# New lists of pieces for the Mamba units of a fused Mamba and mixture-of-experts kernel

## What is computed

```python
def mamba2(u, l):                      # l: layer
    z, xBC, dt = split(u @ in_w[l].T)  # 512, 512 + 64 + 64, 8
    dt  = softplus(dt + dt_bias[l])
    xBC = silu(causal_conv4(xBC) + conv_b[l])
    x, B, C = split(xBC)               # x: 8 heads of 64, B, C: 64
    dA = exp(dt * -exp(A_log[l]))
    state = dA * state + (dt * x) B^T  # over the 512 tokens, per head
    y = state C + D[l] * x
    y = y * silu(z)
    return rmsnorm(y) * rms_w[l] @ out_w[l].T
h = x
for l in range(2):
    h = mamba2(layernorm(h) * ln_w[l] + ln_b[l], l) + h
x = layernorm(x + h)
logits = x @ gate_w + gate_b           # 8 experts, top 2, softmax of the two
x = layernorm(x + sum of w_k * expert_k(x))  # (silu(x Wg) * (x Wv)) @ W2
```

## Time and profile before

| | |
|---|---|
| timed runs | 1418.2, 1421.18, 1423.03 us |
| profiled execution, first to last instruction | 1418.7 us |
| TensorE, VectorE, ScalarE, GpSimd busy | 1272.5, 1090.1, 804.2, 791.7 us |
| plain units | 40.3 and 41.1 us by turns |
| routed units | 44.9 us, one of them 49.8 |
| table loads on ScalarE, lines L1221 and L1210 | 16 and 16 |

### The profile page before, as it was taken

One profiled execution on the slowest core, in us unless ns is written; L12 is line 12 of the kernel. 1 busy time (PEld: TensorE's weight loads), 2 busy tenths in 40 slices (PEclk: granted clock), 3 DMA queues, 4 the chain that ended last, 5 costly groups with the idle time before them and its releaser, 6 DMA issues.

```text
span 1418.7 us, 40444 instructions
## 1 busy us (share of the span) xinstructions
PE 1272.5 (90%) x13336; PEld 1050.7 (74%) x13337; DVE 1090.1 (77%) x2560; ACT 804.2 (57%) x1861; POOL 791.7 (56%) x751
## 2 busy tenths in 40 slices
PE   4889999999999999999888799999999999999970
PEld 2456666666667666666678799999999999999960
DVE  4889999999999999899967877565566656565536
ACT  4667666666666776667545344444454544444436
POOL 3467666767675877788774615234072406152772
PEclk9899999999999999999968999999999999999996
DMA  6213432333443233322235231303012312202594
GB/s 211 81 31 120 135 109 93 96 119 119 135 135 120 84 113 117 123 88 81 87 146 189 72 121 34 121 27 122 30 54 94 105 51 76 72 30 63 134 210 162
DMA packets 90547, 145.73 MB, mean 103 GB/s; under 512 B 9376, under 2 KB 73376, under 8 KB 90336
## 3 DMA queue, kind: packets, MB, share of 16 engines
q1 hardware_dynamic: 75104, 97.03, 21.4%
q0 software_dynamic: 15072, 46.51, 11.2%
q10 hardware_dynamic: 288, 1.19, 0.2%
HBM read 103.03 MB, written 41.67 MB: 102 GB/s over the span
## 4 chain that ended last, share of the span: by engine, by line
PE 48%; DVE 25%; issue 12%; POOL 6%; ACT 5%; DMA 1%; DVEq 1%; SPq 0%; ACTq 0%; POOLq 0%
PE pe L1101 12%; PE pa L1101 12%; PE py L1126 11%; DVE arena L1691 5%; DVE arena L1730 4%; POOL arena L2631 3%; PE pa L676 2%; DVE arena L1738 2%; PE pm L853 2%; PE py L815 2%; DVE arena L1757 2%; DVE arena L1744 1%; PE pt L835 1%; DVE arena L1664 1%; DVE arena L1645 1%
## 5 line engine op out<-in xcount | busy, mean ns | idle before, releaser
L1101 PE MATMUL pe<-arena 128*128 128x128 f16 x3408 | 219.4, 220 | 26.0 <-issue 26.0
L1101 PEld LDWEIGHTS pe<-arena 128*128 128x128 f16 x3408 | 203.4, 98 | 31.3 <-issue 30.6
L1101 PE MATMUL pa<-arena 128*128 128x128 f16 x3408 | 218.8, 220 | 0.0
L1553 ACT ACTIVATE arena<-pe,arena 128x128 f32<-128x128 f32 x568 | 162.0, 371 | 79.8 <-PE pe L1101 78.9
L1101 PEld LDWEIGHTS pa<-arena 128*128 128x128 f16 x3408 | 201.5, 98 | 0.0
L1126 PE MATMUL py<-arena 128*128 (+1 forms) x1704 | 197.7, 273 | 1.3 <-DVE arena L2337 0.9
L1691 DVE SCALAR_TENSOR_TENSOR arena<-pa,arena 128x511 f32<-128x511 f32 (+2 forms) x240 | 178.9, 746 | 11.6 <-ACT arena L1199 5.5
L1126 PEld LDWEIGHTS py<-arena 128*128 128x128 f16 x1704 | 163.4, 98 | 19.6 <-issue 1.8
L2300 DVE SCALAR_TENSOR_TENSOR pm<-pa,arena 128x128 f32<-128x128 f32 x284 | 80.5, 352 | 98.7 <-ACT arena L1553 88.0
L1730 DVE TENSOR_TENSOR_SCAN arena<-arena,pe 128x512 f32<-128x512 f32 x128 | 148.8, 1204 | 3.2 <-issue 1.8
L2531 POOL TENSOR_SCALAR arena<-arena 128x1536 f16<-128x1536 f32 (+2 forms) x35 | 42.6, 1218 | 189.3 <-DVE arena L2337 184.1
(11 more groups left out here) (309 smaller groups left out, 2539.5 us busy)
## 6 DMA issues: line engine op xcount, KB each, us to landing
arena<-step_rows SPq DMA_DIRECT2D x64, 512.0 KB, 6.3
arena<-in_w_exp POOLq DMA_DIRECT2D x32, 768.0 KB, 4.8
arena<-queue SPq DMA_DIRECT2D x74, 129.5 KB, 2.1
answer<-arena SPq DMA_DIRECT2D x71, 128.0 KB, 1.7
arena<-in_x SPq DMA_DIRECT2D x16, 512.0 KB, 6.2
answer<-zeros SPq DMA_DIRECT2D x10, 512.0 KB, 4.8
arena<-h SPq DMA_DIRECT2D x9, 512.0 KB, 5.5
h<-arena SPq DMA_DIRECT2D x8, 512.0 KB, 3.0
```

The lines of the kernel that those rows point to most:

```text
L1101: ins = pe.matmul(bank[:, f * P:(f + 1) * P], w_split[:, p, hl, d * 2 * FF + col:d * 2 * FF + col + P], x[:, r, d, :], start=(n == 0), sto ...
L1553: ins = e.activation(sg[:, half, f, :], GATE[half][:, f * P:(f + 1) * P], ACT.Silu, bias=b1a[:, bass.ds(ex_, 1), ff], scale=1.0 / S1)
```

## The change

Only the order of the calls changes in the functions `plain`, `routed` and `final` on four engines. No piece is added or taken away, and no piece's own code changes. `prologue`, `first`, `epilogue`, SyncE's queue and the expert part stay. Below are the list of `plain` and the parts of `routed` and `final` that matter here, cut from the diff; the printed functions above hold the old lists whole. In `routed`, ScalarE's `x1_apply` now stands behind `conv_silu` of c3 and `z_silu` 0.

On TensorE:

```diff
 def plain(st):
     c = [Chunk(st, k) for k in range(NK + 1)]
-    chunk_a(c[1])
     do_fills(st, ["dt"])
     chunk_cb(c[1])
+    chunk_a(c[1])
     do_fills(st, ["c4"])
     do_fills(st, ["c0"])
     chunk_s(c[0])
...
     steps(st.u + 1, 1 - st.q)
     do_fills(st, ["c1"])
     chunk_c(c[0])
+    chunk_y(c[1])
     chunk_s(c[1])
-    chunk_y(c[1])
+    chunk_a(c[2])
     do_fills(st, ["c2"])
-    chunk_a(c[2])
     chunk_z(c[2])
     chunk_d(c[0])
     chunk_cb(c[2])
     do_fills(st, ["c3"])
+    chunk_c(c[1])
     chunk_s(c[2])
     turn_b(st.u + 1, 1 - st.q, c[0].n + 1)
-    chunk_c(c[1])
     do_fills(st, ["z0"])
+    chunk_a(c[3])
     chunk_y(c[2])
+    chunk_cb(c[3])
+    do_fills(st, ["z2"])
     chunk_d(c[1])
-    chunk_a(c[3])
-    chunk_cb(c[3])
     do_fills(st, ["z1"])
-    do_fills(st, ["z2"])
+    chunk_z(c[3])
     do_fills(st, ["ln0"])
     chunk_c(c[2])
-    chunk_z(c[3])
     chunk_y(c[3])
+    chunk_cb(c[4])
+    do_fills(st, ["ln1"])
     chunk_a(c[4])
-    do_fills(st, ["ln1"])
     chunk_d(c[2])
     chunk_c(c[3])
-    chunk_cb(c[4])
     do_fills(st, ["z3"])
     chunk_d(c[3])
...
 def final(st):
     c = [Chunk(st, k) for k in range(NK)]
     chunk_y(c[0])
+    chunk_s(c[0])
+    chunk_cb(c[1])
     chunk_a(c[1])
-    chunk_cb(c[1])
-    chunk_s(c[0])
+    chunk_z(c[1])
     chunk_c(c[0])
-    chunk_z(c[1])
+    chunk_d(c[0])
     chunk_cb(c[2])
     do_fills(st, ["t0"])
-    do_fills(st, ["t1"])
-    chunk_y(c[1])
-    chunk_d(c[0])
     chunk_a(c[2])
     chunk_s(c[1])
```

On ScalarE:

```diff
 def plain(st):
...
     softplus(st)
     chunk_a(c[1])
     conv_first(st, "c4")
+    first_state(c[0])
     conv_first(st, "c0")
-    first_state(c[0])
+    conv_silu(st, "c4")
+    steps(st)
+    conv_first(st, "c1")
+    squares(c[0])
     chunk_c(c[0])
-    steps(st)
-    conv_silu(st, "c4")
-    conv_first(st, "c1")
+    chunk_a(c[2])
     conv_silu(st, "c0")
-    chunk_a(c[2])
     conv_first(st, "c2")
+    squares(c[1])
     conv_silu(st, "c1")
-    squares(c[0])
     chunk_d(c[0])
     conv_silu(st, "c2")
+    chunk_c(c[1])
     conv_first(st, "c3")
+    z_silu(st, 0)
+    b_rows(st)
+    chunk_a(c[3])
+    ln_apply(st.u + 2, st.q)
+    squares(c[2])
+    z_silu(st, 1)
+    z_silu(st, 2)
+    chunk_c(c[2])
+    ln_out(st, "ln0")
+    conv_silu(st, "c3")
+    chunk_d(c[1])
+    ln_out(st, "ln1")
+    chunk_a(c[4])
+    squares(c[3])
+    chunk_c(c[3])
+    chunk_d(c[2])
+    z_silu(st, 3)
+    chunk_d(c[3])
+
+def routed(st):
+    c = [Chunk(st, k) for k in range(NK + 1)]
+    chunk_a(c[1])
+    softplus(st)
+    conv_first(st, "c4")
+    end_scale(st)
+    first_state(c[0])
+    conv_first(st, "c0")
+    chunk_c(c[0])
+    squares(c[0])
+    conv_silu(st, "c4")
+    chunk_a(c[2])
+    steps(st)
+    conv_first(st, "c1")
+    chunk_d(c[0])
+    conv_silu(st, "c0")
+    chunk_c(c[1])
+    conv_first(st, "c2")
+    b_rows(st)
+    conv_silu(st, "c1")
+    conv_first(st, "c3")
+    chunk_d(c[1])
...
-def routed(st):
-    c = [Chunk(st, k) for k in range(NK + 1)]
-    softplus(st)
-    chunk_a(c[1])
-    conv_first(st, "c4")
-    first_state(c[0])
-    end_scale(st)
-    conv_first(st, "c0")
-    squares(c[0])
-    chunk_c(c[0])
-    steps(st)
-    conv_silu(st, "c4")
-    chunk_d(c[0])
-    chunk_a(c[2])
-    conv_silu(st, "c0")
-    conv_first(st, "c1")
-    conv_first(st, "c2")
-    b_rows(st)
-    chunk_c(c[1])
-    conv_silu(st, "c1")
-    conv_first(st, "c3")
-    x1_apply(st)
-    h_out(st, 0)
```

On VectorE:

```diff
 def plain(st):
     c = [Chunk(st, k) for k in range(NK + 1)]
     scan(c[1])
+    ch1 = Chain(dve, c_dve2, S1_LINKS, st.u + 1)
     dt_first(st)
     chunk_mix(c[1])
-    ch1 = Chain(dve, c_dve2, S1_LINKS, st.u + 1)
     dt_last(st, ch1)
     scan(c[2])
     taps(st, "c4", ch1)
     chunk_b2(c[0])
     chunk_b1(c[1])
+    end_b(st)
     taps(st, "c0", ch1)
-    weigh(st)
-    end_b(st)
     g_low(c[0])
     chunk_b2(c[1])
     next_state(c[1])
...
     chunk_b1(c[2])
     taps(st, "c2", ch1)
     chunk_mix(c[2])
+    next_state(c[2])
+    g_low(c[1])
     ln_stats(st.u + 2, st.h + 1, st.q)
-    g_low(c[1])
     taps(st, "c3", ch1)
     ch1.close()
     chunk_b2(c[2])
-    next_state(c[2])
     scan(c[3])
+    weigh(st)
     chunk_mix(c[3])
     chunk_b1(c[3])
     g_low(c[2])
     chunk_b2(c[3])
     scan(c[4])
+    chunk_mix(c[4])
     g_low(c[3])
-    chunk_mix(c[4])
...
...
     c = [Chunk(st, k) for k in range(NK)]
     scan(c[1])
     chunk_b2(c[0])
+    choose_lead()
     chunk_mix(c[1])
-    choose_lead()
+    g_low(c[0])
+    chunk_b1(c[1])
     end_add(st)
-    chunk_b1(c[1])
-    g_low(c[0])
```

On GpSimd:

```diff
 def plain(st):
+    end(st)
     c = [Chunk(st, k) for k in range(NK + 1)]
+    x_dt(c[1])
+    x_w(c[1])
+    scatter_before(st, 0, 1)
+    gated(c[0])
+    scatter_before(st, 3, 4)
+    old_state(c[1])
+    scatter_before(st, 1, 2)
+    x_d(c[1])
+    scatter_before(st, 5, 6)
+    add_xd(c[1])
+    scatter_before(st, 2, 3)
+    x_dt(c[2])
+    old_state(c[2])
+    gated(c[1])
+    x_w(c[2])
+    x_d(c[2])
+    add_x(st)
+    add_xd(c[2])
+    rsqrt_ln(st.u + 2)
+    x_dt(c[3])
+    scatter_before(st, 6, 7)
+    gated(c[2])
+    x_d(c[3])
+    add_xd(c[3])
+    u_low(st.u + 2, st.q, st, "ln0")
+    scatter_before(st, 4, 5)
+    scatter_before(st, 7, 8)
+    gated(c[3])
+    x_dt(c[4])
+    x_w(c[4])
+    u_low(st.u + 2, st.q, st, "ln1")
+    x_d(c[4])
+
+def routed(st):
+    c = [Chunk(st, k) for k in range(NK + 1)]
+    end(st)
+    x_dt(c[1])
     scatter_before(st, 0, 1)
     x_w(c[1])
     scatter_before(st, 1, 2)
-    scatter_before(st, 2, 3)
+    gated(c[0])
+    scatter_before(st, 5, 6)
     old_state(c[1])
-    end(st)
...
-    c = [Chunk(st, k) for k in range(NK + 1)]
-    end(st)
-    scatter_before(st, 0, 1)
-    scatter_before(st, 1, 2)
-    scatter_before(st, 2, 3)
-    x_w(c[1])
-    x_dt(c[1])
-    gated(c[0])
-    scatter_before(st, 3, 4)
...
 def final(st):
     c = [Chunk(st, k) for k in range(NK)]
...
     gated(c[0])
     x_w(c[1])
     x_dt(c[1])
+    old_state(c[1])
     x_d(c[1])
+    first_weights()
     add_xd(c[1])
-    old_state(c[1])
-    first_weights()
+    old_state(c[2])
+    x_w(c[2])
+    gated(c[1])
     x_dt(c[2])
-    gated(c[1])
-    x_w(c[2])
     x_d(c[2])
-    old_state(c[2])
     rsqrt_x1(st)
     add_xd(c[2])
+    x_dt(c[3])
+    gated(c[2])
+    x_d(c[3])
     scatter_before(st, 0, 2)
-    gated(c[2])
-    x_dt(c[3])
-    x_d(c[3])
     scatter_before(st, 2, 3)
     add_xd(c[3])
     scatter_before(st, 3, 6)
+    scatter_before(st, 6, 8)
     gated(c[3])
-    scatter_before(st, 6, 8)
 def epilogue(st):
```

More of the change, by code:

```diff
@@ new lines, in routed @@
+            def routed(st):
[9 more added lines that the diff above has]
+                conv_silu(st, "c4")
+                chunk_a(c[2])
+                steps(st)
[7 more added lines that the diff above has]
+                conv_first(st, "c3")
+                chunk_d(c[1])
+                squares(c[1])
+                h_out(st, 0)
+                conv_silu(st, "c2")
@@ L1413, in plain @@
                 chunk_a(c[3])
-                z_silu(st, 1)
+                h_out(st, 1)
                 squares(c[2])
                 conv_silu(st, "c3")
+                z_silu(st, 0)
+                x1_apply(st)
+                z_silu(st, 1)
+                ln_apply(st.u + 2, st.q)
                 chunk_c(c[2])
                 z_silu(st, 2)
+                gap_tanh(st)
+                chunk_a(c[4])
                 ln_out(st, "ln0")
-                chunk_a(c[4])
-                ln_out(st, "ln1")
@@ L1466, in routed @@
                 chunk_c(c[3])
                 ln_out(st, "ln1")
-                chunk_d(c[2])
-                squares(c[3])
                 z_silu(st, 3)
@@ L1479, in final @@
                 h_out(st, 0)
+                chunk_a(c[2])
+                squares(c[0])
+                chunk_c(c[1])
+                chunk_d(c[0])
                 h_out(st, 1)
-                squares(c[0])
-                chunk_d(c[0])
-                chunk_a(c[2])
-                chunk_c(c[1])
+                chunk_a(c[3])
                 x1_apply(st)
+                gap_tanh(st)
+                high_parts(0)
+                high_parts(1)
                 squares(c[1])
-                chunk_a(c[3])
-                high_parts(0)
+                chunk_d(c[1])
+                squares(c[2])
                 chunk_c(c[2])
-                squares(c[2])
-                high_parts(1)
-                gap_tanh(st)
-                chunk_d(c[1])
                 e.preload_act_table_set("sqrt_and_others")
+                high_parts(2)
+                squares(c[3])
                 root_out(c[2].q, 0, 3)
                 chunk_c(c[3])
-                squares(c[3])
+                chunk_d(c[2])
                 root_out(c[3].q, 3, NK)
-                chunk_d(c[2])
-                high_parts(2)
             def epilogue(st):
@@ L2022, in routed @@
                 g_low(c[0])
+                ch3 = s3_stats(st)
                 chunk_b1(c[1])
```

(20 more changed lines are left out.)

139 lines of the change are left out of this document (41 added, 98 removed).

## The result

| | before | after |
|---|---|---|
| median of the timed runs | 1419.76 us (1418.2 to 1423.03, 4 runs) | 1473.78 us (1470.98 to 1476.06, 4 runs) |
| ratio to before | | 1.0369, 95% interval 1.0346 to 1.0393 |
| span of the profiled execution | 1418.7 | 1474.4 |
| mean granted clock of TensorE | 0.965 | 0.933 |
| table loads on ScalarE in the Mamba units | 32 | 60 |

What follows compares the result with a forecast made beforehand. A TensorE-VectorE loop, both nearly full, bounds the Mamba units. Plain +6.2, clock +9.6, routed +3.6, final -3 make +16.4; with 1418.7 and 2.5, about 1437 us; range 1413 to 1455.

Steps and rivals of the forecast that it cites:

- So g_low0 waits 1.0: Plain units: VectorE's g_low of chunk 0 waits 1.0 us for ScalarE, held up by a new table load.
- from the end of VectorE's taps c4: Plain units: counted from there, ScalarE needs 6.9 us until g_low of chunk 0 can start, VectorE 5.9.
- rival 3: ScalarE, conv_silu c4 to steps: no load or covered, g_low0's copy within 5.9 us of taps c4; 1412 to 1415, chance 0.17.
- 2.6 was forecast: Plain units: TensorE waits 2.6 us before a2 (transposes of chunk 2), against 0.72 before the change.
- 40.7 + 0.8: Plain unit: +1.1 TensorE, -1.3 VectorE, +1.0 table load make +0.8 us each, +6.2 over eight.
- I take half of the eight: TensorE's clock falls after the wait in half of the eight plain units, 2.4 us each: +9.6.
- rival 2: TensorE's clock falls in every plain unit: 1447 us, up to 1458 where it stays low longer; chance 0.12.
- dense work on both sides of the wait: Plain units: dense work around TensorE's wait spoke against the one row where a similar wait lowered the clock.
- +3.6 was forecast: Six routed units: -0.35 for a wait gone, +0.9 for loads and gated, about +0.6 each; bounds -2 and +8.
- -3 was forecast: Final unit: the last gated on GpSimd comes 2 to 4 us earlier, so -3; bounds -5 and +2.
- choose_lead goes ahead of mix1: Final unit: with this, first_weights is issued some 4 us sooner, but GpSimd's last gated sets the end.
- no scan waits for a step row: Routed units: step rows go out some 8 us later, yet land 5 us before the next unit's scan1.

Runs made afterwards that it cites:

- e4: The changed kernel with ScalarE's steps ahead of conv_silu c4 in the plain and routed lists, so the 28 extra table loads go: 1473.35 us, ratio 1.0354.
- e5: The changed kernel with TensorE computing s1 (chunk_s of chunk 1) six times instead of once in each plain unit: 1450.79 us, ratio 1.0187.
- e8: The changed kernel with GpSimd's plain wait for end_b (1443.39 us), plus TensorE's steps and cb of chunk 2 back ahead of z1 in routed: 1433.9 us.
- e9: The changed kernel with GpSimd's plain wait for end_b, plus TensorE's s1 ahead of fills c1 and c2 in routed: 1444.29 us, ratio 1.0176.

## Why the prediction was wrong, point by point

- **The direction, slower, was right; its main reason was wrong.** "So g_low0 waits 1.0" for ScalarE's table load. The 28 loads came as forecast, but g_low waits nothing, and without them the time is the same (e4). The step that failed is the count "from the end of VectorE's taps c4" with conv_silu c4 at 3.24, load included: ScalarE had nothing left to do at 237.34, so the load ahead of Silu ran beside the taps, which ended at 238.59. Only the load before the Exp counts, and the 6.9 us were 5.6 (to 244.15), less than VectorE's 5.9. That was rival 3's condition, and it held.
- **A term was missing: the price of a moved piece beside its new neighbour.** VectorE's end_b was entered at its old 2.60, while its place and that of three GpSimd products were both moved. It took 4.53. The trace before could have warned: the 2.68 of the earlier trace rows already stood beside an add, which took 1.50 where 1.27 is usual. The +1.0 put down to the loads and the +1.93 of the contention (4.53 for 2.60) act at the same place, so the timetable came out near by luck: a wait of 3.2 at a2, where 2.6 was forecast, and 41.6 for a unit at full clock (e5), where 40.7 + 0.8 was.
- **The clock: mechanism right, size too small.** "I take half of the eight", 2.4 us each, +9.6. It fell in all eight, rival 2, and cost 2.7 in each of the six middle ones, 21.1 in all by e5's profile; e5 gave back 23. The argument that dense work on both sides of the wait would hold the clock had no row behind it. Rival 2's 1447 with the two misses below, 15 and 10, is 1472; but that sum hides that rival 2, too, had a load in g_low's way and no collision.
- **Routed units: +3.6 was forecast, +18.6 measured.** The step counted ScalarE's loads and a delay of 0.1 to 0.2 by GpSimd's gated. It never asked what TensorE had done in gated's time, though the prediction's own show the one long wait of this kind, 2.61 at c(0) before 569.22. The list took steps and cb2 out of that place, and in two units dt_last now stands 1.67 us longer beside x_w, which no term held either; so the one long wait became three. e8 puts steps and cb2 back and gains 9.5, half of the 18.6. The collision's share is read from the trace (a wait of 2.78 with it, 1.03 without) and was not tested by a run.
- **Final unit: -3 was forecast, +7.3 measured.** "choose_lead goes ahead of mix1" was named and given no price. It is 5.15 us of VectorE in front of g_low of chunk 0, and TensorE's d0 waits 3.60 for that. The estimate also had no term for the clock, and the 7.3 are that term: behind this wait TensorE ran 30.7 us at half clock. In e9, where it did not, the same list took 52.9, 3.1 less than the 56.0 of before. That does not confirm the -3, for e9's final unit had 20.9 us at half clock and that of before 34.1.
- **Right:** no scan waits for a step row. They leave SyncE by 585.9 and take 6.5 to land, 4 us before the next unit's scan at 596.42; 5 were forecast. The waits before weigh (265.23) and before g_low of chunk 3 (273.51) are gone.
- **The range** ended at 1455 because rival 2's 1458 was its only bad case. It kept routed and final at their forecast values; their own upper bounds, +8 and +2, were not added to it, and both were too low.

What stays open: what a routed list without dt_last's collision would take, and what decides whether a wait is followed by half clock, above all in the final unit.

## What to carry to other kernels

When a list is reordered, enter each piece at the price that it has beside its new neighbours, not at its old one: a VectorE instruction on two SBUF operands and a GpSimd product shut each other out, and one wait that parts them can be worth more than the idle time that it adds. Then go through TensorE's waits and ask of each piece taken out of one what covers it now, because the wait can cost a second time at half clock: here one of 3.2 us cost 2.7 more. Before a table load, a queue or a copy is put on the path, look whether its engine is idle at the moment from which you count.
